# The product of delta*u with B in a selective scan: on DVE at the head of each step in place of POOL a step ahead

## The reference

```python
def step(h, inp):
    d_t, u_t, b_t, c_t = inp
    dA = jnp.exp(d_t[..., None] * A)
    h = dA * h + (d_t * u_t)[..., None] * b_t[:, None, :]
    y = jnp.einsum('bdn,bn->bd', h, c_t)
    return (h, y)
...
y = selective_scan(u, delta, A, Bm, Cm) + u * D
y = y * jax.nn.silu(z)
return y @ out_proj_w.T
```

## Time and profile before

| what | us |
| --- | --- |
| median of 3 runs (range) | 1881.72 (1878.11 to 1881.87) |
| profiled execution: span; the median lies 9.0 above it | 1872.7 |
| busy in the whole span: PE / PE weight load | 1398.0 (75%) / 644.1 (34%) |
| DVE | 1081.3 (58%) |
| ACT | 897.9 (48%) |
| POOL | 541.5 (29%) |
| POOL's products, L442, x128, in the program | 408.4 |
| DVE's scans, L885, x256 | 474.0 |

### The profile page before, as it was taken

The page is one execution under the profiler, slowest core; times in us unless marked ns, Lnnn a source line. Parts: engine busy times, 40 slices in busy tenths (PEclk is TensorE's granted clock), DMA queues, the critical chain, the costliest instruction groups (busy, mean ns, idle before and its releaser), DMA issues.

```text
span 1872.7 us, 15244 instructions
## 1 busy us (share of the span) xinstructions
PE 1398.0 (75%) x5491; PEld 644.1 (34%) x5491; DVE 1081.3 (58%) x1089; ACT 897.9 (48%) x1136; POOL 541.5 (29%) x182
## 2 busy tenths in 40 slices
PE   6254555668556677466796449999999998889999
PEld 2121122224222243123454222232222323448888
DVE  5999999999999999999608220010100101644001
ACT  4332224344333523343022339989989894563210
POOL 0654636555465555566305200000000000000000
PEclk8676668778778887777888659999999997999999
DMA  5010110111010111011105980000000000010611
GB/s 185 23 45 23 46 45 23 44 45 47 22 45 28 40 46 43 25 45 45 46 0 73 105 86 1 1 1 1 1 0 0 0 0 1 1 45 1 271 44 45
DMA packets 26411, 74.32 MB, mean 40 GB/s; under 512 B 2627, under 2 KB 13123, under 8 KB 23700
## 3 DMA queue, kind: packets, MB, share of 16 engines
q1 hardware_dynamic: 26356, 73.63, 15.2%
HBM read 60.05 MB, written 2.36 MB: 33 GB/s over the span
## 4 chain that ended last, share of the span: by engine, by line
DVE 40%; PE 35%; issue 10%; ACT 8%; DMA 4%; SPq 1%; POOL 1%; DVEq 0%; ACTq 0%; POOLq 0%
DVE arena L885 16%; PE ps L1535 8%; PE ps L1520 8%; DVE arena L895 8%; ACT arena L713 5%; PE ps L1644 3%; DMA arena<-arena 3%; PE ps L1685 3%; DVE arena L875 2%; DVE arena L820 2%; DVE arena L824 2%; PE ps L1673 1%; PE ps L1662 1%; PE ps L1254 1%; SPq L388 1%
## 5 line engine op out<-in xcount | busy, mean ns | idle before, releaser
L442 POOL TENSOR_TENSOR arena<-arena 128x1024 f32<-128x1024 f32 x128 | 408.4, 3192 | 406.2 <-DVE arena L885 307.1
L885 DVE TENSOR_TENSOR_SCAN arena<-arena 128x512 f32<-128x512 f32 x256 | 474.0, 1865 | 2.5 <-POOL arena L442 2.5
L1313 PE MATMUL ps<-arena,ident 128*128 128x512 f32 x432 | 274.2, 776 | 233.8 <-DVE arena L895 122.7
L713 ACT ACTIVATE arena<-ps,bound 128x1024 f32<-128x1024 f32 (+1 forms) x416 | 420.7, 1213 | 26.0 <-PE ps L1520 26.0
L565 ACT ACTIVATE arena<-arena 128x512 f32<-128x512 f32 x256 | 169.5, 713 | 509.4 <-DVE arena L885 429.1
L1520 PE MATMUL ps<-arena 97*128 (+3 forms) x832 | 218.2, 384 | 22.2 <-issue 20.1
L1313 PEld LDWEIGHTS ps<-arena,ident 128*128 128x128 f32 x432 | 95.6, 238 | 387.9 <-DVE arena L895 168.7
L1535 PE MATMUL ps<-arena 128*32 128x512 f32 (+1 forms) x1664 | 222.5, 607 | 1.1 <-ACT arena L713 0.9
L1147 DVE COPY arena<-ps 128x512 f32<-128x512 f32 x16 | 11.1, 691 | 353.6 <-PE ps L1535 353.6
L430 POOL TENSOR_TENSOR rstd<-ve,mhalf 128x4 f32<-128x4 f32 (+3 forms) x18 | 30.7, 1707 | 587.3 <-DVE ve L1172 467.7
L895 DVE TENSOR_TENSOR arena<-arena 128x1024 f32<-128x1024 f32 x128 | 159.6, 1246 | 0.1
(11 more groups left out here) (183 smaller groups left out, 1544.9 us busy)
## 6 DMA issues: line engine op xcount, KB each, us to landing
arena<-bc_scratch SPq DMA_DIRECT2D x64, 512.0 KB, 4.4
arena<-in_mw SPq DMA_DIRECT2D x16, 1024.0 KB, 9.4
arena<-arena SPq DMA_DIRECT2D x48, 128.0 KB, 14.8
arena<-arena SPq DMA_DIRECT2D x12, 400.2 KB, 16.8
arena<-in_w SPq DMA_DIRECT2D x2, 1024.0 KB
out<-xt SPq DMA_DIRECT2D x4, 512.0 KB, 2.9
xt<-in_x SPq DMA_DIRECT2D x1, 1536.0 KB
arena<-in_ctx SPq DMA_DIRECT2D x1, 1200.8 KB, 7.5
```

The lines of the kernel that those rows point to most:

```text
L442: pool.tensor_tensor(dbu[:, w % 2], du[:, 2 * p:2 * p + 2], over(bg[:, q % 2, n % BG], 2), ALU.mult).then_inc(S["dbu_ready"], 1)
L713: act.activation(flat(prob[0:n, v % 2, 2 * h:2 * h + 2]), ps[0:n, 2 * (r % 3):2 * (r % 3) + 2, :].rearrange("p a b -> p (a b)"), ACT.Exp, ...
L885: dve.tensor_tensor_scan(state(w)[:, x], da[:, w % AHEAD, x], dbu[:, w % 2, x], carry[:, d, n:n + 1], ALU.mult, ALU.add).then_inc(S["scan_ ...
L1313: last = mm(bank(2 * p + x), ident[:, :], state(2 * j + s)[:, x], start=False, stop=(j >= NP - DP and (j in SUMMED or s == 1)))
```

## The change

`scan_input` moves from POOL's program to DVE's. Its wait for `scan_done` goes, since the scans that read the buffer stand ahead of it on the same engine; the waits for `du` and for the load of B stay. DVE makes the first product of a chunk ahead of its first scan, and then product w + 1 behind the scans of step w and ahead of the multiplication by C of step w - 1. POOL keeps the pair additions and the roots.

```diff
@@ gpsimd
-            def scan_input(c, w, first=False):
-
-                (n, p), q = step(w), w // (BG * DP)
-                if w == 0:
-                    pool.wait_ge(S["du_ready"], c + 1)
-                if w % (BG * DP) == 0:
-                    pool.wait_ge(bc_in[q % 2], c * 16 * NBG + 32 * (q // 2 + 1))
-                if w >= 2 or not first:
-                    pool.wait_ge(S["scan_done"], c * 2 * NU + 2 * (w - 1))
-                pool.tensor_tensor(dbu[:, w % 2], du[:, 2 * p:2 * p + 2], over(bg[:, q % 2, n % BG], 2),
-                                   ALU.mult).then_inc(S["dbu_ready"], 1)
...
             def scan_chunk(c, first=False, second=False, last=False):
                 for w in range(NU):
-                    scan_input(c, w, first)
                     if w % 2 == 0 and w // 2 - 2 in SUMMED:
                         add_pair(c, w // 2 - 2)
@@ vector
+            def scan_input(c, w):
+
+                (n, p), q = step(w), w // (BG * DP)
+                if w == 0:
+                    dve.wait_ge(S["du_ready"], c + 1)
+                if w % (BG * DP) == 0:
+                    dve.wait_ge(bc_in[q % 2], c * 16 * NBG + 32 * (q // 2 + 1))
+                dve.tensor_tensor(dbu[:, w % 2], du[:, 2 * p:2 * p + 2], over(bg[:, q % 2, n % BG], 2),
+                                  ALU.mult).then_inc(S["dbu_ready"], 1)
...
             def scan_chunk(c, first=False, second=False, last=False):
 
+                scan_input(c, 0)
                 for w in range(NU):
                     scan(c, w, first)
+                    if w + 1 < NU:
+                        scan_input(c, w + 1)
                     if w >= 1:
                         times_c(c, w - 1)
```

## The result

| | kernel before | changed kernel |
| --- | --- | --- |
| median of the runs, us (range) | 1880.17 (1878.11 to 1881.87, 4 runs) | 1775.46 (1773.51 to 1776.65, 4 runs) |
| profiled span, us | 1872.7 | 1774.9 |
| first scan's start to last scan's start, us | 56.3 to 905.8: 849.5 | 55.1 to 801.5: 746.4 |
| start of the last multiplication by C, us | 908.3 | 804.0 |

The changed kernel takes 0.9442 of the time (95% interval 0.9428 to 0.9455): 105 us less, where 107 were forecast. That is why the spans differ by 98 only; the scan, which the change touches, became 104.3 us shorter (908.3 to 804.0).

The account below looks back on a forecast made before the run. DVE bounds the scan, busy 847.2 of 850 us, part of it blocked by POOL's SBUF reads. -286 + 37 + 143 - 2.5, taken as -107, gives span 1765.7; plus 9.0 the median, 1775 us; range 1763 to 1803.

Parts of the forecast that it names:

- Blocking removed: In the scan, POOL's SBUF-reading operations stretch DVE's instructions by 286 us in all; 37 of it stays with the pair additions.
- Additions kept: The 20 pair additions left on POOL still block DVE, up to 42 us, taken as 37.
- The third rival: Pair additions on POOL cost DVE more than now, 3.35 us each, 67 in place of 37: 1805 us; 4 in 100.
- Products added: 128 products on DVE in the scan at 1.12 us each, start to start: 143 us, all on the path.
- The first wait: DVE's one wait for POOL's first product, 2.5 us in the scan, goes away.
- The sum: -286 + 37 + 143 - 2.5 = -108, taken as -107 with 1 us for dependent gaps at four chunk heads.
- The span and the 9.0 us: Profiled span forecast at 1765.7 us; the median's 9.0 above the span before added at the end: 1774.7.
- ACT, PE and the load of B: Costed at nothing: ACT 43% and PE 74% of a 188 us middle chunk; B's load of 4.3 us has 11.8.
- ACT's densest piece: Two steps of decays among Silus and Gelus take 11.4 us, DVE 9.4; ACT or PE late, say 1811; 8 in 100.
- The dependent gap: Between a product and the scan reading it, expected at a chunk's head only: 1 us for four heads.
- The rival that trusted the share: DVE's long scans are its own work, so the added 143 us make it slower: 2022 us; 3 in 100.
- A product held for its whole record: If POOL's products held the port for their recorded 408 us, the sum would be about 1651 us; rejected from the trace.

Follow-up runs that it names:

- One: Changed kernel with no product of delta*u and B at all, its buffer zeroed once ahead of the scan: 1630.95 us, scan 603.7.
- two: Kernel before, with POOL writing zeros (a memset of 128x1024) in place of making each product: 1632.0 us, scan 603.9.
- Four: Kernel before, with POOL making each product twice, the second behind the first: 2144.78 us, scan 1113.7.
- five: Changed kernel with the products of odd steps back on POOL, even ones staying on DVE: 1827.01 us, scan 798.7.
- eight: Changed kernel without POOL's 20 pair additions, PE summing all states itself: 1735.83 us, again 1728.93; ratio to before 0.9198.
- six: Changed kernel with each product directly ahead of the scan that reads it, not one step ahead: 1787.52 us, scan 760.7.
- nine: Changed kernel without pair additions, ten products back on POOL beside DVE's gate products, statistics and step sizes, which were moved up: 1722.58 us, ratio to before 0.9178.

## Why the prediction was right

For the scan it was right in mechanism and in size; for the span it was not as exact as the median looks. By its own steps:

- *Blocking removed.* Forecast 286 - 37 = 249 from 128 products. One shows 245.8 (849.5 - 603.7), and two 245.6. The prediction's reading, mean less unblocked time, was within 2%. Four and five price a product on POOL at 2.01 and 1.94, where I had 2.10 uncovered and 1.93 on the average.
- *Additions kept.* Forecast 37, measured 38 (eight). In the changed kernel's scan just 20 instructions of DVE are stretched, one for each addition: 6 scans, 8 carry copies, 3 of the input norm and 3 of the convolution (L811). The third rival would have needed more. The reading of PE's wait of 30.4 us for an addition as queueing behind POOL's products was not borne out: without the products the longest is still 26.4, and the ten waits add up to 81.5 us where there were 111.0. No scan waited for it.
- *Products added.* Forecast 128 x 1.12 = 143, measured 142.7 (one). The start-to-start distance was the right price; the record's 1.19 would have given 152.
- *The first wait.* Forecast 2.5. The first scan starts at 55.1 in place of 56.3, 1.2 sooner, because the first product stands there now; that product was among the 128, so this agrees.
- *The sum.* -245.8 + 142.7 - 1.2 = -104.3, which is by how much the scan's end came sooner, against -107. The blocking term is the one that was off, by 3 us. Smaller still: from the start of the multiplication by C to the next start are 1.13 us where they were 1.12, which is half of the 0.02 that the plain step is longer than forecast.
- *The span and the 9.0 us.* The span was forecast at 1765.7 and came out at 1774.9: 2.7 us of the 9.2 are the scan's, 6.5 the part behind it, which was longer than in the profile of before (969.7 against 963.2). The median was forecast 9.0 above the span, but a profiled execution's time lies only 1.8 above its span here. As far as the record shows, the 9.0 was mostly the distance from the profiled execution of before to the median of before; it made up for the span by chance.
- *ACT, PE and the load of B.* No scan waited for them: 0.2 us of idle time ahead of all 256 scans. ACT's densest piece did not show. A middle chunk became 194 to 198 us long, not 188; 215 was a stretch within one of 220 to 223. The dependent gap was rightly kept to a chunk's head; were it in every step it would be 14 us (six).
- *Occupancy as a measure.* DVE was 99.7% busy and got 143 us more work, and the kernel became 5.6% faster: 246 us of its busy time in the kernel before was waiting for products inside records, and some 38 more for additions. The rival that trusted the share would have had 2022; four shows that the long records follow POOL's work.
- *A product held for its whole record.* The 1651 us that the prediction sets beside its own figure mixes two counts: the 408 us are the products' alone, so the 37 for additions is not to be added back, and by that reading the sum is 1881.7 - 408 + 143 - 2.5 = 1614. Measured were 1775, so the rejection stands.

That the forecast median, 1775, was met within 1 us is luck: the part behind the scan varies by more than that, and two misses of about 9 and 7 us cancelled. What the runs bear out is the scan, to 3 us in 104.

## What to carry to other kernels

A busy record need not be work: compare an instruction's mean or maximum with its shortest. Where the surplus is the same for a copy of two elements and a scan of 512, and its end is the end of another engine's instruction, price the other engine's work by that surplus. In this kernel a product on POOL was free only where DVE read PSUM or made the statistics for as long as POOL took. Having one input is not the condition: copies and the convolution's first product have one tensor input from SBUF and were held too (0.138 to 2.264 and 0.539 to 2.576 in the earlier trace rows). Elsewhere the work belongs on the saturated engine itself, when that engine makes it in less than the hold (1.12 against 1.9 us here), or nowhere, as the pair additions that spared an engine with room. Then order it so that no instruction needs the one right ahead of it.

## What was not expected

- A memset of 128x1024 on POOL (0.95 us) beside two-input DVE instructions cost nothing measurable, 1632.0 against 1630.95 us with no POOL product at all; the expectation had left room for up to 28 us.
- A POOL product that starts undisturbed is recorded with 2.35 us, and DVE is held up to its end; the stretches of 2.1 come from products recorded with about 3.2, which start while DVE is still in an instruction. To cover one takes DVE work of that length: 3.6 us were enough, 2.26 left 0.22, and 1.39 were worth almost nothing (nine).
- The best of these kernels, nine and eight, take 0.918 and 0.920 of the time of before, 2.6 to 2.9% less than the change alone (0.9447, run beside them). Most of it came from leaving out the 20 additions that were meant as help.
